# First feed-forward of a four-layer decoder in the form of the last: second product turned, second bias on partitions, router beside the first products

## The reference

```python
# x = x + ffn(layernorm(x)); 1792 tokens of 256, 1024 hidden, 8 "experts", top 2
router_logits = xt @ router_w                                   # 256 -> 8
router_probs = softmax(router_logits)
top_k_probs, top_k_indices = top_k(router_probs, 2)
top_k_probs = top_k_probs / sum(top_k_probs)
combine = einsum('tk,tke->te', top_k_probs, one_hot(top_k_indices, 8))
expert_out = gelu(xt @ w1 + b1) @ w2 + b2                       # one shared expert
out = expert_out * sum(combine, axis=-1)
```

## Time and profile before

| | us |
|---|---|
| median of 3 runs | 3066.73 |
| lowest, highest | 3066.44, 3071.94 |
| the profiled execution's own time | 3068.3 |
| span of its trace | 3066.6 |
| PE busy | 2623.7 (86% of the span) |
| DVE, ACT, POOL busy | 1443.6, 1294.5, 891.2 |
| mean granted clock of TensorE | 0.92 of full speed |

### The profile page before, as it was taken

One profiled execution on the slowest core, in us unless ns is written; L12 is line 12 of the kernel. 1 busy time (PEld: TensorE's weight loads), 2 busy tenths in 40 slices (PEclk: granted clock), 3 DMA queues, 4 the chain that ended last, 5 costly groups with the idle time before them and its releaser, 6 DMA issues. The chain is left out here.

```text
span 3066.6 us, 55571 instructions
## 1 busy us (share of the span) xinstructions
PE 2623.7 (86%) x18272; PEld 1882.0 (61%) x18273; DVE 1443.6 (47%) x3490; ACT 1294.5 (42%) x3858; POOL 891.2 (29%) x572
## 2 busy tenths in 40 slices
PE   5746999979787989999599877899959997988899
PEld 2335666656455556666489734566649996876554
DVE  5695888931534234444522376666650003553200
ACT  1334677832443123333233222677733332772222
POOL 3264455510001022222133243455522222330000
PEclk8867999979898999999799987999979998998999
DMA  2000000000241010000367600000045554004100
GB/s 105 1 0 28 17 20 20 16 30 0 58 105 52 0 45 21 15 15 15 126 207 237 204 33 33 22 15 20 15 181 171 177 184 134 1 17 113 56 12 13
DMA packets 108488, 194.38 MB, mean 63 GB/s; under 512 B 56532, under 2 KB 81060, under 8 KB 96596
## 3 DMA queue, kind: packets, MB, share of 16 engines
q1 hardware_dynamic: 93986, 166.80, 16.9%
q0 software_dynamic: 6816, 18.62, 2.1%
q10 hardware_dynamic: 7570, 7.47, 0.8%
HBM read 174.16 MB, written 18.71 MB: 63 GB/s over the span
## 5 line engine op out<-in xcount | busy, mean ns | idle before, releaser
L1438 POOL TENSOR_TENSOR L_xattn_p<-L_xattn_p,L_xattn_ri 112x1500 f32<-112x1500 f32 (+1 forms) x192 | 436.0, 2271 | 566.2 <-DVE L_xattn_ri L1746 566.2
L1651 ACT ACTIVATE L_xattn_pT<-ps 125x448 f32<-125x448 f32 (+1 forms) x576 | 256.5, 479 | 358.4 <-PE ps L1542 357.8
L1542 PEld LDWEIGHTS ps<-ident,L_xattn_p 112*125 112x125 f32 x1920 | 255.8, 191 | 121.2 <-ACT L_xattn_pT L1651 41.7
L1542 PE MATMUL ps<-ident,L_xattn_p 112*125 112x112 f32 x1920 | 292.0, 284 | 41.8 <-POOL L_xattn_p L1438 29.1
L1663 ACT ACTIVATE L_xattn_p<-L_xattn_sa,L_xattn_ng 112x375 f32<-112x375 f32 x512 | 304.8, 601 | 16.4 <-DVE L_xattn_ng L1762 10.7
L1093 PEld LDWEIGHTS ps<-L_ffn_xsT,L_ffn_w 128*128 128x128 f32 x2240 | 265.4, 195 | 7.0 <-issue 1.9
L1093 PE MATMUL ps<-L_ffn_xsT,L_ffn_w 128*128 128x128 f32 x2240 | 266.5, 278 | 2.4 <-ACT L_ffn_xsT L1123 2.4
L276 POOL TENSOR_TENSOR ln_rstd<-ln_tmp,half 112x8 f32<-112x8 f32 x26 | 44.4, 1722 | 703.7 <-DVE ln_tmp L225 526.5
L1155 DVE TENSOR_TENSOR L_ffn_y<-ps,L_ffn_pack 128x256 f32<-128x256 f32 x70 | 29.7, 425 | 365.4 <-PE ps L1102 365.4
L1102 PE MATMUL ps<-L_ffn_weights,L_ffn_hT 128*128 x840 | 192.9, 379 | 2.3 <-DVE L_ffn_hT L1167 2.3
L1564 PE MATMUL ps<-L_xattn_kT,L_xattn_qm 32*112 32x375 f32 (+1 forms) x1280 | 173.3, 524 | 11.2 <-DVE L_xattn_ng L1759 5.8
(11 more groups left out here) (415 smaller groups left out, 5113.2 us busy)
## 6 DMA issues: line engine op xcount, KB each, us to landing
L_ffn_w<-in_L_ffn_experts SPq DMA_DIRECT2D x74, 1024.0 KB
L_xattn_src<-in_ctx SPq DMA_DIRECT2D x48, 375.0 KB, 3.0
L_attn_toeplitz<-L_attn_h SPq DMA_DIRECT2D x4, 3136.0 KB, 24.0
L_ffn_weights<-in_L_ffn_experts SPq DMA_DIRECT2D x8, 1028.0 KB, 17.2
L_xattn_keys<-in_ctx SPq DMA_DIRECT2D x16, 281.2 KB, 6.0
L_xattn_rows<-in_ctx_rows SPq DMA_DIRECT2D x16, 281.2 KB
L_ffn_weights<-in_L_ffn_experts SPq DMA_DIRECT2D x8, 516.0 KB, 8.7
L_ffn_w<-in_L_ffn_experts SPq DMA_DIRECT2D x4, 1026.0 KB, 9.5
```

The costliest lines, as they stand in the source:

```text
L1438: g.tensor_tensor(P[:, m % 4, :, :], P[:, m % 4, :, :], ri[:, m % 4, :].unsqueeze(2).broadcast_to([T, W, S2]), ALU.mult).then_inc(s["prob_ ...
L1542: last = pe.transpose(turned(t)[:, j * T:(j + 1) * T], P[:, m % 4, j, kc * KW:(kc + 1) * KW], k.ident[0:T, 0:T])
L1651: act.activation(PT[:, m % 4, kc, :, :].rearrange("p h t -> p (h t)"), turned(t), ACT.Copy).then_inc(s["pt_ev_a"].sem, 1)
```

## The change

The first feed-forward goes to `joint_experts` too, with one expert, so 8 steps a group and 32 in all. `sub_ffn` loses its other branch, `router` is split into parts (`router_parts`) that can be put into another block, and `add_second_biases` is gone. For the first feed-forward, `joint_experts` now

- asks `layer_norm` for the router's products and loads the expert as before,
- runs `choose` and `weigh` on DVE at the start of the block, beside PE's first steps, and the exponential on ACT before the gelu of step 6 (`t == per_group - 2`),
- applies gelu with b1 as it is, lifts with b2 on partitions,
- multiplies by the token's gate while adding to X, one sequence at a time, and takes the next norm's statistics,
- does not write the output.

The host lays b2 out as two columns on 128 partitions in place of one row of 256.

```diff
 def sub_ffn(k, ctx, name, packs, spec):
...
-    gates = k.tile(ctx, name + "_gates", [T, spec["experts"] * B], F32)
-    slots, load_first = expert_slots(k, ctx, name, edram, elay, spec["experts"])
-    layer_norm(k, pack=(tile, dram, lay["_total"]), ahead=load_first, router_w=chunks(p("router"), 2))
-    router(k, ROUTED, None, gates, spec["mode"])
-    add_second_biases(k, gates, 1, p("b2"))
-    feed_forward(k, name, edram, slots, elay, spec["experts"], KP, spec["hidden"], spec["gated"], spec["act"], gates)
+    joint_experts(k, ctx, name, (tile, dram, lay["_total"]), p, elay, edram, spec)
...
-    layer_norm(k, pack=pack, ahead=load_all)
+    fixed = spec["mode"] == "fixed"
+    layer_norm(k, pack=pack, ahead=load_all, router_w=None if fixed else chunks(p("router"), 2))
...
+    by_token = sb("by_token", [T, B])
+    if not fixed:
+        exponentials, choose, weigh = router_parts(k, ctx, ROUTED, None, by_token, spec["mode"])
...
             for t in range(steps):
                 g, e, m = place(t)
-                if g == 0 and m == 0:
+                if fixed and g == 0 and m == 0:
                     act.wait_ge(*gate_v.at(e + 2))
+                if not fixed and t == per_group - 2:
+                    exponentials(act)
                 act.wait_ge(*up.at(t + 1))
                 act.wait_ge(*down.at(t - RING + 1))
...
+                    act.activation(hT[:, t % RING, :], k.ps[:, t % 2, 0:GT], spec["act"],
+                                   bias=part(e, "b1")[:, m:m + 1]).then_inc(acted.sem, 1)
...
+            else:
+                choose(v, ch)
+                weigh(v, ch)
+            second = b2 if fixed else p("b2")
             for g in range(G):
                 v.wait_ge(*down.at((g + 1) * per_group))
                 v.wait_ge(*turned.at(2 * (g - 1)))
                 for half in range(2):
-                    v.tensor_scalar(oT[:, g % 2, half, :], k.ps[:, 4 + 2 * (g % 2) + half, 0:GT], b2[:, half:half + 1],
+                    v.tensor_scalar(oT[:, g % 2, half, :], k.ps[:, 4 + 2 * (g % 2) + half, 0:GT], second[:, half:half + 1],
                                     None, ALU.add).then_inc(lifted.sem, 1)
...
+                    for j in range(2):
+                        b = g * GB + 2 * r + j
+                        last = v.scalar_tensor_tensor(k.x(b), k.ps[0:T, 2 + r, j * D:(j + 1) * D], by_token[:, b:b + 1],
+                                                      k.x(b), ALU.mult, ALU.add)
+                    last.then_inc(added.sem, 1)
+                    v.wait_ge(*added.at(2 * g + r + 1))
+                    for j in range(2):
+                        k.moments(v, g * GB + 2 * r + j)
...
-        small = dict(router=in_lanes(w["router_w"]), b2=w["b2"][None])
+        small = dict(router=in_lanes(w["router_w"]), b2=columns(w["b2"]))
```

More of the change, by code:

```diff
@@ L492, in router @@
 def router(k, E, bias, gates, mode):
-    nc = k.nc
     with ExitStack() as ctx:
[L501 to L510, removed]
+        exponentials, choose, weigh = router_parts(k, ctx, E, bias, gates, mode)
@@ L511, in _ @@
+        with k.nc.Block(no_gpsimd_drain=True) as block:
             @block.scalar
@@ L519, in _ @@
                 ch = Chain(v, k["vec_step"])
[L520 to L547, removed]
-                    ch.link(v.tensor_tensor(ex[:, :, :], ex[:, :, :], ahead[:, :, :], ALU.mult))
-                    ch.link(v.tensor_reduce(one[:, :], ex[:, :, :], AX.X, ALU.add))
-                    ch.link(v.reciprocal(inv[:, :], one[:, :]))
-                    if mode == "softmax_topk":
-                        ch.link(v.tensor_tensor(g3, ex[:, :, :], inv[:, :].unsqueeze(2).broadcast_to([T, B, E]),
-                                                ALU.mult))
[L554 to L557, removed]
@@ L741, in _ @@
         def _(sp):
-            for g in range(G):
+            for g in range(G if fixed else 0):
                 sp.wait_ge(*added.at(2 * g + 2))
@@ L793, in _ @@
         def _(act):
-            act.wait_ge(*gate_v.at(1))
-            act.activation(gates[:, :], gates[:, :], ACT.Exp).then_inc(gate_a.sem, 1)
+            if fixed:
+                act.wait_ge(*gate_v.at(1))
+                act.activation(gates[:, :], gates[:, :], ACT.Exp).then_inc(gate_a.sem, 1)
             k.table(act, spec["act"])
@@ L831, in _ @@
                     v.wait_ge(*turned.at(2 * g + r + 1))
[L832 removed]
+                    if fixed:
+                        v.tensor_tensor(x, k.ps[0:T, 2 + r, 0:2 * D], x, ALU.add).then_inc(added.sem, 1)
+                        continue
+                    for j in range(2):
[6 more added lines that the diff above has]
+                        k.moments(v, g * GB + 2 * r + j)
             ch.close()
[L834 to L835 removed]
+    k.advance(up_mm=steps, up_act=steps, down_mm=steps, gs_copied=2 * G, gt_tr=2 * G, down_added=2 * G, gate_v=X + 1 if fixed else 1,
+              gate_a=1, **{n: 16 for n in ("exp_in0", "exp_in1", "toep_in0", "toep_in1")[:X]})
 FFN = {
```

141 lines of the change are left out of this document (78 added, 63 removed).

## The result

Four runs after the change have a median of 3030.58 us (3027.65 to 3032.95), four of the kernel before beside them 3067.14 (3066.44 to 3071.94). The ratio is 0.9882, with a 95% interval of 0.9869 to 0.9894. That is 36.6 us less; I had reckoned 31.8 less and given a range that begins at 3031. The direction was right and the range was missed by 0.4 us, less than two medians of this kernel differ (3030.58 here, 3031.92 in the run "again", which lies inside it).

What follows compares the result with a forecast made beforehand. PE was taken to bound the first feed-forward, behind a serial chain of router and second biases. 27.0 + 7.0 + 2.4 - 2.6 - 2.0 = 31.8 us less, so 3066.7 - 31.8 = 3035 us, range 3031 to 3040.

Steps and rivals of the forecast that it cites:

- Part 1: First feed-forward's start: router and second biases leave the path, PE's first product starts at 651.62, 27.0 us less.
- Rival 2: Router in the first feed-forward not hidden, PE or ACT waits for its gates: 3036 to 3043 us, chance 0.06.
- Parts 2 and 3: First feed-forward's products: second product turned, 7.0 us less; six turns back among the steps, 2.6 us more.
- Part 4: First feed-forward's start: PE's slow start at the clock's lower level goes, 2.4 us less.
- rival 1: PE's clock falls at the first feed-forward's start, keeping back 2.4 us of gain: 3037.4 us, chance 0.20.
- Part 5: First feed-forward's tail, last product to DVE's last statistics: 5.26 us in place of 3.24, 2.0 us more.
- The sum: First feed-forward from router's first instruction to next norm: 31.8 us less, 104.7 in place of 136.5.
- Rival 3: PE's clock stays at the lower level through the whole first feed-forward block: 95 us more, 3130 us, chance 0.02.
- What could be late next: Stage after the first feed-forward: shifts as a whole, with no formerly covered transfer now waited for.
- what goes from this stretch goes from the whole time: First feed-forward: no other stage runs beside it, so its whole saving, 31.8 us, counts in the total.

Runs made afterwards that it cites:

- again: The changed kernel timed and profiled once more, no edit, against the kernel before: 3031.92 us, ratio 0.9887.
- not_turned: The changed kernel with the second product as before (256 columns moving, no lift or turns), b2 left out: 3034.33 us, ratio 0.9894.
- pe_waits_choice: The changed kernel with one more wait: PE's first product waits until the router's choice is made: 3039.69 us, ratio 0.9913.
- matched: no_second_bias with twice as many satisfied waits as filled at the program's start, on five engines: 3049.52 us, ratio 0.9953.
- no_second_bias: The kernel before without its block of second biases, b2 left out of the result: 3044.92 us, ratio 0.9928.
- filled: no_second_bias with already satisfied waits on five engines in the program's first microseconds, 67 instructions more: 3043.50 us, ratio 0.9924.
- filled_dve: no_second_bias with 12 satisfied waits (6 instructions) on VectorE alone at the program's start: 3051.65 us in one run, 3044.45 when timed again.
- router_apart: The changed kernel with the router's choice, exponential and weighing in their own block ahead of the products: 3042.84 us, ratio 0.9921.

## Why the prediction was off, point by point

- **Part 1** (27.0): right. First product 0.16 after DVE's first instruction where I put 0.12. The gates were ready at 669.16, said "about 669"; table loads at 665.04 and 666.67, said "near 666"; no wait of PE behind gelu 6. Rival 2 fell.
- **Parts 2 and 3** (7.0 and 2.6): right. A turn pushes the next product back by 0.44 (L744 at 740.05, L723 at 740.49). From 650.59 to 749.67 PE takes 99.1 us, where 256 x 0.3763 + 2.64 = 99.0; not_turned confirms the net.
- **Part 4** (2.4): right; rival 1 fell. The clock stayed up over the pause of 0.57. In the windows of the kernel after, it is 1.00 at 645 to 646, when PE had run nothing but the norm's transposes since 640.64. The Trainium skill, "TensorE: Matmul & The Clock Gate", section "Part 4: PE-mode transpose", says of a transpose that "it doesn't count as PE-busy the same way". By that rule the start would have been slow, as it is in pe_waits_choice after 5.32 us of pause; this trace disagrees with it.
- **Part 5** (2.0): right. From 749.67 to 754.96 are 5.29 us, said 5.26.
- **The sum**: 104.9 measured, 104.7 said; from norm to norm 31.7 less, said 31.8. Rival 3 fell.
- **The step that failed** is "What could be late next", with its sentence that the next stage "shifts as a whole", and before it "what goes from this stretch goes from the whole time". I looked there only for transfers that would be waited for and found none, rightly. I put at nothing what the edit does to stages behind it, whose code then stands elsewhere. By matched the place of the code is worth 4.6 to 6.0 us in the medians (4.1 to 6.3 in the table's rests), less up to 0.6 for the waits themselves. From before to after the rests fell by 4.7. Of these, 3.0 lie in the third routed feed-forward, in every profile: as long as in matched, and short in no_second_bias and filled, so they go with the code's place, though filled_dve was once as long by chance, and the changed kernel was not run with its code at before's place. The others are not shown to: 1.8 lie in the first attention, ahead of the change (269.2, 267.7 and 269.3 us before, 268.2 and 265.7 after), and are scatter. So 3067.1 - 31.7 = 3035.4 by the stretch, some 3 less by the place of the code in all likelihood, and up to 2 less by chance, against 3030.6 and 3031.9 measured. The kernel before happened to stand badly; this part of the gain is no merit of the change's idea.
- **The range**: for untouched stages I gave a scatter of 1 to 2 us and no case for a shift of them. Two profiles of one kernel differ there by 2.6, and those of filled_dve by 8. Both runs of after lie at the low end, one 0.4 outside and one inside, so which side of the end they fell on is luck; a shift of 3 us or more on top of that scatter asked for a range that reaches lower.

## What to carry to other kernels

Work on short chains that leave the bounding engine idle is worth most when it is moved beside products that need none of it: 29 of the 32 us came so (17.8 by no_second_bias, 11.3 by router_apart), and only 2.5 from the cheaper form of the products. A sum over one stretch can be right to 0.2 us and the whole still off by 5, some 3 of it here because the edit moved later code and the rest scatter; before crediting or blaming an edit for a few microseconds, cut the traces at common marks and compare the untouched stages. To tell an edit's own effect from that of the code's place, put as many idle instructions as the edit took away where the engines wait anyway, and count in the trace how many they became.

## What was not expected of the hardware

- 134 idle instructions in the program's first microseconds make the kernel before without its second biases 4.6 us slower than it is without them, of which at most 0.6 is spent there; 67 of another mix do not (3043.50 against 3044.92). A pause of 0.24 us in "issue" reappears at the same instruction; with half as many on VectorE a shorter one stands at the same place of the stream, on an instruction six later.
- The level of the clock makes a small delay large, and not in every execution: the same 32 matmuls take 6.56 or 5.05 us in two executions of one kernel, when they start 0.26 us later in the stage.
- A change of the table on ACT costs 1.28 with 0.02 around it (665.04, 666.34, 666.65 to 666.67). Two of them and an exponential take 2.94 between two gelu; as a step leaves ACT idle for 2.37, one gelu is 0.56 late, and the next is on time again (670.41) without a wait of PE.
